# Attention with a gated branch on one core: the two early low parts of w in one piece ahead of the norms, and other orders around wo and in the last two units

## The reference

```python
xn = _layernorm(x, axis=-1)
# attention: b = 2, s = 512, H = 32, HKV = 8, HD = 128
q = _rmsnorm(heads(xn @ Wq.T), q_norm_w)
k = _rmsnorm(heads(xn @ Wk.T), k_norm_w)
v = heads(xn @ Wv.T)
scores = jnp.einsum('bkgqd,bksd->bkgqs', qg, k) / math.sqrt(HD)
bias = jnp.where(rel > 0, NEG_INF, slopes[:, :, None, None] * rel)
attn = jax.nn.softmax(scores + bias[None], axis=-1)
s = jnp.einsum('bkgqs,bksd->bkgqd', attn, v) @ Wo.T
# gate
low = jnp.einsum('bsd,hrd->bshr', xn, A)
g = silu(SCALING * jnp.einsum('bshr,hor,bsh->bso', low, B, H * softmax(xn @ Wr.T + br)))
y = x + s * g
```

## Time and profile before

| what | value |
|---|---|
| time, median of 3 runs | 783.61 us (783.03 to 785.84) |
| the profiled execution | 785.95 us, of which the span from first to last instruction is 784.1 us |
| TensorE matmuls busy | 733.6 us (94%) |
| VectorE busy | 623.4 us (79%) |
| ScalarE busy | 562.3 us (72%) |
| GpSimd busy | 367.8 us (47%) |
| mean granted TensorE clock | 0.976 |

### The profile page before, as it was taken

How to read it: one execution, slowest core, us unless ns; L and a number is a source line. 1 busy time by engine, 2 the same in 40 slices (tenths; PEclk the granted TensorE clock), 3 DMA queues, 4 the chain that set the end, 5 groups by cost and what they waited for, 6 DMA issues and landing times.

```text
span 784.1 us, 14644 instructions
## 1 busy us (share of the span) xinstructions
PE 733.6 (94%) x3741; PEld 619.7 (79%) x3741; DVE 623.4 (79%) x1467; ACT 562.3 (72%) x1440; POOL 367.8 (47%) x343
## 2 busy tenths in 40 slices
PE   8888989999999989999899989999899998999867
PEld 7776878887788778888788778888788787888746
DVE  7855788798878889698887888787886888878873
ACT  4665778697677778777776876777786976779662
POOL 5314354456234643554344743544544553347275
PEclk9999999999999999999999999999999999999989
DMA  8014958678595857779595867859586785957731
GB/s 288 0 28 112 264 146 229 191 221 229 144 277 141 243 169 217 206 188 272 126 271 150 229 182 186 262 145 269 142 228 184 220 235 127 285 141 202 219 119 67
DMA packets 214773, 148.02 MB, mean 189 GB/s; under 512 B 48992, under 2 KB 205536, under 8 KB 214624
## 3 DMA queue, kind: packets, MB, share of 16 engines
q1 hardware_dynamic: 214752, 147.77, 66.8%
HBM read 85.84 MB, written 61.87 MB: 188 GB/s over the span
## 4 chain that ended last, share of the span: by engine, by line
issue 41%; POOL 25%; PE 18%; DVE 6%; ACT 1%; POOLq 1%; DVEq 0%; ACTq 0%
POOL pt_lo L549 13%; POOL inv_rms L539 8%; POOL wo_lo L533 3%; DVE w_lo L1035 2%; PE qkv_ps L1259 2%; PE qkv_ps L1261 2%; PE qkv_ps L1260 2%; PE turn_ps L1259 2%; POOL inv L543 2%; PE out_ps L1259 1%; PE turn_ps L1260 1%; PE turn_ps L1261 1%; PE out_ps L1260 1%; PE out_ps L1261 1%; PE score_ps L1259 1%
## 5 line engine op out<-in xcount | busy, mean ns | idle before, releaser
L549 POOL TENSOR_TENSOR pt_lo<-x_sb,pt_hi 128x512 fp32r<-128x512 f32 x137 | 175.5, 1304 | 256.6 <-ACT pt_hi L730 256.6
L667 ACT ACTIVATE probs<-probs,neg_max 128x128 f32<-128x128 f32 (+3 forms) x256 | 141.8, 556 | 65.3 <-DVE neg_max L946 64.5
L946 DVE CUSTOM_DVE_ANT_0 probs<-score_ps,cst,slope 128x128 f32<-128x128 f32 (+3 forms) x256 | 129.6, 546 | 56.5 <-PE score_ps L1261 42.0
L675 ACT ACTIVATE probs<-probs,recip 128x128 f32<-128x128 f32 (+3 forms) x252 | 126.3, 549 | 20.4 <-DVE recip L953 20.4
L1259 PE MATMUL qkv_ps<-w_hi,xt_hi 128*128 128x256 f32 (+1 forms) x396 | 130.3, 329 | 4.9 <-DVE squares L1020 3.4
L1260 PE MATMUL qkv_ps<-w_lo,xt_hi 128*128 128x256 f32 (+1 forms) x396 | 129.8, 328 | 0.0
L1261 PE MATMUL qkv_ps<-w_hi,xt_lo 128*128 128x256 f32 (+1 forms) x396 | 129.4, 327 | 0.0
L539 POOL TENSOR_TENSOR inv_rms<-sums,minus_half 128x5 f32<-128x5 f32 x64 | 78.6, 1229 | 98.6 <-DVE sums L1004 98.6
L1259 PE MATMUL out_ps<-wo_hi,o_hi 128*128 128x512 f32 x252 | 102.5, 407 | 5.3 <-DVE o_lo L990 5.3
L967 DVE STREAM_TRANSPOSE squared<-probs 128x256 f32<-128x256 f32 (+3 forms) x124 | 101.9, 822 | 1.4 <-ACT probs L675 0.3
L1260 PE MATMUL out_ps<-wo_lo,o_hi 128*128 128x512 f32 x252 | 100.7, 400 | 0.0
(11 more groups left out here) (176 smaller groups left out, 1605.9 us busy)
## 6 DMA issues: line engine op xcount, KB each, us to landing
turning_qk<-qk_squared SPq DMA_DIRECT2D x240, 80.0 KB, 1.9
qk_moved<-turning_qk SPq DMA_DIRECT2D x60, 320.0 KB, 3.3
turning<-squared SPq DMA_DIRECT2D x120, 128.0 KB, 2.4
x_sb<-turning SPq DMA_DIRECT2D x30, 512.0 KB, 5.0
w_raw<-wqkv SPq DMA_DIRECT2D x32, 384.0 KB, 5.2
turning<-squared SPq DMA_DIRECT2D x120, 96.0 KB, 2.0
x_sb<-turning SPq DMA_DIRECT2D x30, 384.0 KB, 4.3
turning<-squared SPq DMA_DIRECT2D x128, 64.0 KB, 1.8
```

The source lines that it names most:

```text
L549: nc.gpsimd.tensor_tensor(by_quad(pt_lo, j), moved_block(t, j), by_quad(pt_hi, j).bitcast(F32), ALU.subtract).then_inc(pt_lo_by_pool, 1)
L667: nc.scalar.activation(probs[:, h, 0:n], probs[:, h, 0:n], ACT.Exp, bias=neg_max[:, h:h + 1], scale=-1.0, accum_out=total[:, h:h + 1]).the ...
L675: nc.scalar.activation(to[:, h, 0:n], probs[:, h, 0:n], ACT.Copy, scale=recip[:, h:h + 1]).then_inc(probs_ready, 1)
L946: nc.vector.tensor_tensor_reduce(probs[:, h, 0:n], score_bank(t, h), cst[:, C_DIST + SEQ - n:C_DIST + SEQ], slope[:, h:h + 1], HUGE, ALU.a ...
```

## The change

In words:

1. VectorE's `w_slot`: in a slot with weights due it makes the low parts of pieces 0 and 1 in one go, ahead of `normalize_k`. Before, piece 0 was there and piece 1 came after `normalize_q` and the first reciprocals. `set_factor` goes from between the two norms to the end of the slot. In the last group's slot 5 (no weights due) `turned_qk_lo` of unit 6 goes to the front of `normalize_k`; on ScalarE `turned_qk_hi` of unit 6 goes in front of the first `normalize_probs` there.
2. GpSimd's `split_w` first waits until VectorE has made both of its low parts.
3. ScalarE makes all four high parts of wo behind all four `normalize_probs` of the slot; before, two came ahead of the second pair.
4. The last two units: the order of steps changes on ScalarE, VectorE and TensorE (see the diff). `gate_tangents` and `multiply_gate` of blocks 4 to 7 are cut in two: 4 and 5 early, 6 and 7 late. On TensorE `scores` of the last unit come ahead of an `out`, and all four `turn_probs` of it ahead of the next. GpSimd finishes 4 blocks of y, not 3, ahead of `start_last_y`.

```diff
             def split_w(group, chunks=range(KC)):
+
+                pool.wait_ge(w_lo_by_dve, group * EARLY_W)
                 for c in chunks:
...
             def end(g):
                 turned_lo(g, BY_PE - 1)
                 pool.wait_ge(x_again, 16 * BLOCKS)
-                for m in range(3):
+                for m in range(4):
                     finish_y(m)
                 start_last_y()
-                for m in range(3, BLOCKS - 2):
+                for m in range(4, BLOCKS - 2):
                     finish_y(m)
...
+                if left == 1 and t == W_SLOT:
+                    turned_qk_hi(g, t + 1)
                 if here(t, left):
                     normalize_probs(g, t, range(0, 2))
                 if left == 1 and t < W_SLOT:
                     gate_tangents(range(2 * (t - 3), 2 * (t - 3) + 2))
-                if here(t + 1, left):
+                if here(t + 1, left) and not (left == 1 and t == W_SLOT):
                     turned_qk_hi(g, t + 1)
-                if wo_due:
-                    act.wait_ge(out_ready, ONE(g, t - 2, 0))
-                    split_wo(g + t // BLOCKS, range(0, 2))
                 if here(t, left):
                     normalize_probs(g, t, range(2, HPG))
                 if wo_due:
-                    split_wo(g + t // BLOCKS, range(2, HPG))
+                    act.wait_ge(out_ready, ONE(g, t - 2, 0))
+                    split_wo(g + t // BLOCKS, range(0, HPG))
...
                 exponentials(g, before, range(0, HPG))
-                mixed_hi(g, before - 2, 1)
                 turned_qk_hi(g, last)
 
                 for pair in range(2):
                     act.wait_ge(probs_written[pair], WRITTEN(g, before, 0))
                 normalize_probs(g, before, range(0, 2), late_probs)
+                mixed_hi(g, before - 2, 1)
                 normalize_probs(g, before, range(2, HPG), late_probs)
                 moved_hi(g, before - 1)
-                gate_tangents(range(4, BLOCKS))
+                gate_tangents(range(4, 6))
                 exponentials(g, last, range(0, 3))
...
                 normalize_probs(g, last, range(2, HPG))
+                gate_tangents(range(6, BLOCKS))
                 mixed_hi(g, before, 1)
...
                 moved_lo(g, t - 2)
                 if w_due:
-                    split_w(g + 1, range(0, 1))
+                    split_w(g + 1, range(0, EARLY_W))
+                else:
+
+                    turned_qk_lo(g, t + 1)
                 normalize_k(g, t + 2)
-                if w_due:
-                    set_factor(g, t + 3)
                 normalize_q(g, t + 2)
                 reciprocals(g, t, 0)
-                if w_due:
-                    split_w(g + 1, range(1, EARLY_W))
                 square_both(g, t + 2)
                 reciprocals(g, t, 2)
                 add_out(g, t - 3)
                 square_probs(g, t, 0)
-                turned_qk_lo(g, t + 1)
+                if w_due:
+                    turned_qk_lo(g, t + 1)
                 square_probs(g, t, 2)
                 mixed_lo(g, t - 2, left)
+                if w_due:
+                    set_factor(g, t + 3)
...
                 reciprocals(g, before, 2)
+                turned_qk_lo(g, last)
                 add_out(g, before - 3)
                 mixed_lo(g, before - 2, 1)
-                turned_qk_lo(g, last)
-                multiply_gate(range(4, BLOCKS))
-                add_out(g, before - 2)
                 for h in range(3):
                     bias(g, last, h, at_end=True)
+                multiply_gate(range(4, 6))
+                add_out(g, before - 2)
                 mixed_lo(g, before - 1, 1)
+                for n in range(keys_of(before)):
+                    turned_lo(before, n)
                 bias(g, last, 3, at_end=True)
                 reciprocals(g, last, 0)
-                for n in range(keys_of(before)):
-                    turned_lo(before, n)
                 reciprocals(g, last, 2)
                 add_out(g, before - 1)
                 mixed_lo(g, before, 1)
+                multiply_gate(range(6, BLOCKS))
                 for n in range(keys_of(last)):
                     turned_lo(last, n)
...
                 mix(g, before - 2, 1)
-                out(g, before - 2)
                 for h in range(3):
                     scores(g, last, h)
+                out(g, before - 2)
                 mix(g, before - 1, 1)
                 for n in range(keys_of(before)):
                     turn_probs(before, n)
                 scores(g, last, 3)
                 out(g, before - 1)
                 mix(g, before, 1)
-                for n in range(2):
+                for n in range(keys_of(last)):
                     turn_probs(last, n)
                 out(g, before)
-                for n in range(2, keys_of(last)):
-                    turn_probs(last, n)
                 last_mix(g, last)
                 last_out(g, last)
```

## The result

The changed kernel takes 763.13 us (median of 4 runs, 760.81 to 764.28). The kernel before, run beside it, takes 783.32. The ratio is 0.9735, with a 95% interval of 0.970 to 0.9769. The profiled execution takes 764.28 us, with a span of 762.5.

The account below looks back on a forecast made before the run. TensorE was taken as the bound, with w-slot waits and half clock behind them. 23.1 us (3.3 in 7 slots) plus 3.0 for wo less 1.5 at the end gave 24.6 us off, so 760 us, range 749 to 771.

Parts of the forecast that it names:

- the copy: Last VectorE step of the w slot (set_factor), exposed beside GpSimd's pt_lo: 0.5 us charged per slot, from 0 to 0.6.
- the end: Last group's slot 5 and last units: net 1.5 us lost, between 3 us gained and 5 us lost.
- the clock: TensorE behind each w slot: the half-clock stretch goes, 1.6 us back per slot.
- wo: Slot 10: GpSimd's wo parts start later, TensorE's wait for k's low part goes, 3.0 us gained in all.
- What bounds the kernel: TensorE, with 2.6 us waits for VectorE's late low part of w and half clock behind them; GpSimd holds VectorE.
- The w slot's steps: VectorE's two low parts back to back, GpSimd's pair 1.0 us later, TensorE's wait 0.4 us instead of 2.6.
- the two chains: At the end: TensorE's own chain ends about 3 us earlier, GpSimd's last step moves from 774.95 to about 781.
- The stop stays long enough to cost the clock: Rival in the w slots: waits of 1.5 and 1.3 us still lower the clock; around 771, 784 at worst; chance 0.13.
- Slower: Rival in the w slots: GpSimd's two parts each end 2 us later, TensorE waits 4.4 us; 795; chance 0.04.

Follow-up runs that it names:

- e1: The kernel before with VectorE's new w-slot order and GpSimd's wait for both low parts, nothing else changed: 759.95 us, ratio 0.9674.
- e3: The kernel before with GpSimd's wait alone, VectorE keeping its old order: 768.77 us, ratio 0.9787.
- e2: The kernel before with VectorE's new w-slot order alone, without GpSimd's wait: 758.62 us, ratio 0.9668.
- e7: The changed kernel with q and k of unit 6 split where they were before in the last group's slot 5: 759.52 us.
- e9: The changed kernel with four useless VectorE sums between its two low parts in the w slots: 779.53 us.
- e4: The kernel before with ScalarE's four high parts of wo behind all four norms, nothing else: 788.45 us, ratio 1.0018.
- e12: The changed kernel with k's low part ahead of the first square_probs and o's ahead of the second in slots 3, 7, 11: 765.50 us.

## Why the prediction held, and where it did not

- **Size.** Forecast 760 us in 749 to 771, measured 763.13. The sum was 24.6 us off the profiled execution; its span gave up 21.6. Part of this closeness is luck: the terms below were off in both directions, the copy by 3.5 us and the end by 1.4 to the good, the clock by some 2.8 and wo by some 5 to the bad.
- **What bounds the kernel**: right. The waits and the half clock behind them made up the gain: e1, which touches nothing else, has all of it. The cause named (VectorE held beside GpSimd) is shown by e3, where GpSimd's absence alone makes the same two instructions 0.16 and 0.94 us.
- **The w slot's steps**: right to a tenth or two. Forecast and found, in the third slot: both parts done 1.9 us after they start (1.81), GpSimd's added wait 1.0 (0.98), TensorE's wait for piece 3 0.4 (0.32), the end of k's low part, shifted by the 5.4 us, 283.4 (283.35).
- **The copy at the slot's end**: the 0.5 us charged for it was not due. GpSimd's `pt_lo` ended at 284.52, the copy ran from 284.48 in 0.15 us. I had `pt_lo` start at 289.1, which is 283.7 here; it started at 283.22. The exposure that I charged for is real: in e2, where `pt_lo` ended 0.34 us after the copy's start (282.05 and 281.71), the copy took 0.36 us.
- **The clock**: no half clock behind any of the seven w slots, as forecast. 7.3 us of matmul time in six periods is 1.2 per slot; I had read 1.6 from one stretch.
- **The wo order**: the step that failed, 3.0 us credited. The wait that I removed went as forecast (2.9 to 0.4), but two others grew from 1.9 to 6.3 us together: some 2 us lost where 3.0 were credited. The prediction saw GpSimd end its parts 0.7 us later and checked only `out`, which uses them. It did not follow what else is queued behind them: GpSimd's norm step, for which VectorE waits in the next slot, and ScalarE's `o_hi`. Forecast were 3.7 us per group (3.3 and 0.43), found 3.07 in the six periods; wo is the term that lies between them, since the w slot's own terms come to 3.5 as found (2.6 less 0.34, and 1.2 of clock).
- **The end**: forecast 1.5 us lost, found 0.1 lost. The mechanism was the forecast one: VectorE idle 2.48 us in front of q_lo (about 3 forecast), TensorE 2.77 and 3.83 us, GpSimd's last step at the close. So were the two chains: shifted by the 21.6 us, VectorE's last step, behind TensorE, ended 2.9 us earlier than before (757.46 here, 782.01 before; "about 3" forecast), and GpSimd's 5.2 us later (forecast 6). Undoing the early q and k gave 3.6 us (e7), near the 3.9 us by which I had moved the norms.
- **The rivals.** "The stop stays long enough to cost the clock" did not come about: the waits stayed short. That a stop of 1.3 us would have cost the clock, as that rival had it, is not borne out by e9 (full clock behind 1.30 to 1.63 us in all seven w slots). "Slower" needed GpSimd's two parts to end 2 us later each; they took the same 3.66 us as before.

GpSimd's last row shows the close of the span: it ends at 758.58, and the stores follow to 762.5. The chain that ended last goes through GpSimd's steps there, where in the kernel before it went through TensorE and VectorE's `last_y`.

```profile
757.26 1.32 POOL L560 TENSOR_TENSOR acc<-acc,w_raw 128x512 f32<-128x512 f32 x1
```

## What to carry to other kernels

Where a small instruction takes ten times its usual time, look at what the neighbour engine runs beside it; to move the critical one ahead, where it starts first, was worth more here (24 us) than to hold the other back (14 us), which made the other's own product late and moved the collision to the next step. When steps are moved later on an in-order engine, follow every step queued behind them, not only the consumer of what was moved: a stop that is removed in one slot comes back in the next where that engine's next product is late. And an operand split ahead of other work is only early if its input is: ask what its own wait will hold.

## What the runs showed of the hardware

- One stop of TensorE of 2.56 to 2.70 us was followed by a stretch at half clock in all seven w slots of the kernel before. Stops of 1.30, 0.32 and 0.47 us close together were not (e9), and nor were single ones of 2.57 us (e4, seventh w slot) and 2.77 us (changed kernel, last units), while one of 1.95 us was (e12, last units).
- In e2 GpSimd's first low part grew from 1.84 to 2.58 us when VectorE's started first; in the kernel before it was VectorE's that grew, from 0.95 to 2.00. A copy of 128x5 elements took 1.60 us beside GpSimd's part and 0.15 us without it (changed kernel).
